# A token table from one-hot matmuls in place of scattered rows, with attention written out by group number and a lead of units that grows from 6 to 18

## What is computed

```python
x = L0_attn_x
x = x + layernorm(attention(layernorm(x)))
x = x + layernorm(ffn(layernorm(x)))

# attention: 16 heads of 16, keys and values from a latent of 64, causal
attn = softmax(where(causal_mask, -inf, einsum('bhtl,bsl->bhts', q_lat, c_kv) / sqrt(hs)))

# ffn: top 2 of 8 experts for each of the 4096 tokens
w, idx = top_k(xf @ Wg, 2);  w = softmax(w)
xhat = (xf - mu) * rsqrt(var + EPS)
h = relu((xhat * gamma[e] + beta[e]) @ W1[e] + b1[e])
out[e] = h @ W2[e] + b2[e] + xf
y[n] = sum over the two chosen e of w[n, e] * out[e][n]
```

## Time and profile before

| | us |
|---|---|
| median of 3 runs | 1285.25 (1284.64 to 1285.45) |
| the profiled execution | 1283.42 |
| its span, first to last instruction | 1281.8 |
| TensorE busy | 1054.5 (82%) |
| VectorE busy | 824.1 (64%) |
| ACT busy | 640.9 (50%) |
| POOL busy | 588.2 (46%) |

### The profile page before, as it was taken

One profiled execution on the slowest core, in us unless ns is written; L12 is line 12 of the kernel. 1 busy time (PEld: TensorE's weight loads), 2 busy tenths in 40 slices (PEclk: granted clock), 3 DMA queues, 4 the chain that ended last, 5 costly groups with the idle time before them and its releaser, 6 DMA issues. The chain is left out here.

```text
span 1281.8 us, 24447 instructions
## 1 busy us (share of the span) xinstructions
PE 1054.5 (82%) x7329; PEld 806.4 (63%) x7329; DVE 824.1 (64%) x2492; ACT 640.9 (50%) x1111; POOL 588.2 (46%) x675
## 2 busy tenths in 40 slices
PE   5979999999999999998533513999999999999900
PEld 2545555555555555554233513999999999999900
DVE  6739877777777777772188521556655655565577
ACT  2640666666666666666444422444444544454533
POOL 4214555555555555556747771223222222232237
PEclk9985999999999999999855555999999999999955
DMA  4994344545444444432261235142541414421173
GB/s 147 372 359 131 107 167 167 167 167 167 165 165 160 159 160 160 169 113 108 96 236 66 83 128 196 59 162 63 183 178 48 177 49 177 146 79 50 41 270 131
DMA packets 93849, 190.03 MB, mean 148 GB/s; under 512 B 27480, under 2 KB 58600, under 8 KB 85512
## 3 DMA queue, kind: packets, MB, share of 16 engines
q1 hardware_dynamic: 84508, 165.14, 37.0%
q0 software_dynamic: 7680, 22.09, 5.0%
q10 hardware_dynamic: 1588, 1.92, 0.5%
HBM read 109.54 MB, written 79.05 MB: 147 GB/s over the span
## 5 line engine op out<-in xcount | busy, mean ns | idle before, releaser
L778 ACT ACTIVATE att_pt<-att_ps_s 128x1024 f32<-128x1024 f32 (+3 forms) x384 | 297.9, 814 | 180.5 <-PE att_ps_s L693 176.8
L805 DVE CUSTOM_DVE_ANT_0 att_ps_m<-att_ps_m,keep_future 128x384 f32<-128x384 f32 (+2 forms) x384 | 204.3, 586 | 77.9 <-PE att_ps_m L656 77.9
L1521 ACT ACTIVATE moe_hf<-moe_ps_h,moe_b 128x256 f32<-128x256 f32 x288 | 134.4, 474 | 224.7 <-PE moe_ps_h L1477 215.3
L656 PE MATMUL att_ps_m<-att_k,att_q 128*128 128x512 f32 (+3 forms) x576 | 181.1, 389 | 5.1 <-DVE att_pm L805 3.9
L814 DVE TENSOR_REDUCE att_pm<-att_ps_m 128x1 f32<-128x512 f32 x256 | 161.4, 685 | 21.8 <-PE att_ps_m L656 21.7
L601 POOL TENSOR_SCALAR_AFFINE_SELECT att_pt<-att_pt 128x512 f32<-128x512 f32 x128 | 81.3, 636 | 186.8 <-ACT att_pt L778 186.8
L693 PE MATMUL att_ps_s<-att_q,att_k 128*128 128x512 f32 (+3 forms) x576 | 156.0, 360 | 6.3 <-ACT att_pt L778 5.2
L1430 POOL DMA_INDIRECT ys<-moe_o,moe_home x72 | 74.1, 1029 | 183.3 <-DVE moe_o L1560 170.4
L693 PEld LDWEIGHTS att_ps_s<-att_q,att_k 128*128 128x128 f32 x576 | 95.2, 188 | 56.5 <-issue 28.9
L1554 DVE TENSOR_TENSOR moe_hTl<-moe_hf,moe_hTh 128x256 fp32r<-128x256 f32 x288 | 124.1, 431 | 10.0 <-DVE moe_hTh L1552 0.2
L656 PEld LDWEIGHTS att_ps_m<-att_k,att_q 128*128 128x128 f32 x576 | 99.7, 195 | 47.9 <-DVE att_pm L805 15.1
(11 more groups left out here) (197 smaller groups left out, 2503.8 us busy)
## 6 DMA issues: line engine op xcount, KB each, us to landing
att_raw<-in_w SPq DMA_DIRECT2D x16, 1024.0 KB, 5.3
ws<-att_raw_hi SPq DMA_DIRECT2D x16, 1024.0 KB, 3.9
ws<-att_raw SPq DMA_DIRECT2D x16, 1024.0 KB, 5.8
moe_rows<-xs SPq DMA_DIRECT2D x38, 258.0 KB
att_q<-qs SPq DMA_DIRECT2D x33, 256.0 KB
att_k<-ks SPq DMA_DIRECT2D x66, 128.0 KB
weights_w_0h<-ws SPq DMA_DIRECT2D x8, 1024.0 KB
weights_w_0l<-ws SPq DMA_DIRECT2D x8, 1024.0 KB
```

Source lines behind the costliest of these rows:

```text
L656: ins = pe.matmul(out[:, end - keys:end], qg[slot][:, h // 2, i * P:(i + 1) * P], kg[slot][:, h, k0:k0 + keys], start=not whole, stop=not ...
L778: act.activation(pt[:, blk % NPT, 2 * p:2 * p + 2, off:CH], ps_s[k % 2][:, :, off:CH], ACT.Exp, scale=HS ** -0.5).then_inc(ex_done, 1)
L805: ins = dve.tensor_tensor_reduce(part, part, future[:, CH - keys:CH], 1.0, LOWEST, ALU.add, ALU.max, pm[:, g % 2, 0, head, place:place + 1])
L1521: act.activation(hf[:, f % NHB], ps_h[f % NHB][:], ACT.Relu, bias=b1[r][:, f:f + 1]).then_inc(hf_done, 1)
```

## The change

In words:

- attend is written out for 16 groups with constant numbers, without the loop over b and without registers. The turn is one job, and the lead of units of the next group is AHEAD = (6, 10, 14, 18): 6 before the first scores, and `DEALT_RISE` deals 42 units instead of 38 in each of the groups 0, 1 and 2. Three slots are left (NSL = 3), and the load of group g+2 is issued in group g. The first fetch of raw weights comes behind the load of group 2.
- route makes no slots. `route_xf` and `route_xh` come from ACT straight out of the attention's result (L1214 and L1220), with the turned copies between them; one set of moments of x and its normalised copy on VectorE are gone. The rows are written to HBM in the order of the tokens, by plain DMAs of SP. Rank and expert become a row and a column: per batch and choice POOL makes one-hot matrices (`make_low`, 16 of 128 columns, L946; `make_block`, 16 of 272 columns, L952), ACT scales the first ones by the token's number (`rows_of`, L1237 and L1239), and TensorE multiplies the two (`table`, 32 matmuls of 272 columns a batch), so that a PSUM bank holds for every expert and place the token that belongs there. For the last batch VectorE makes the low ones and half of the others. VectorE makes `home` and `token` of the table.
- experts: POOL reads the tile's column of the table and fetches the rows by two indirect DMAs, in front of the stores of the tile before; its places come by one copy from `home`. SP issues only biases and fills.

```diff
-NSL = NG
+NSL = 3
-HALF = NU // 4 * 2
+AHEAD = (6, 10, 14, 18)
+DEALT_RISE = ((2, 0), (1, 2), (1, 0), (2, 0), (2, 0), (1, 1), (2, 0), (1, 0), (2, 0), (1, 3), (2, 0), (2, 0),
...
-        extra = {7: [("out", 0, 0)], 15: [("out", 0, 1)], 17: [("turn", 1, 0), ("turn", 1, 1)]}.get(k, [])
...
+    first = [*units[:NU], ("turn", 0, 0), *units[NU:NU + AHEAD[0]]]
...
+                for g in range(GROUPS):
+                    if 0 < g < GROUPS - 2:
+
+                        sp.wait_ge(pv_done, g * NB)
+                        load_group(sp, d, slots, g + 2)
+                    if g + 1 < GROUPS:
+                        max_rows(g + 1)
+                    keep_split(g)
```

```diff
+        def make_low(eng, b):
...
+            for k in range(K):
+                for t in range(TB):
+                    ins = eng.tensor_scalar(at_low[:, k, t], cols[:, 0:P], low[:, k, t:t + 1], None, ALU.is_equal)
+            ins.then_inc(low_done, 1)
...
+        def make_block(eng, k):
...
+            for t in range(TB):
+                ins = eng.tensor_scalar(at_block[:, k, t], cols[:], cell[:, k, t:t + 1], None, ALU.is_equal)
+            ins.then_inc(block_done, 1)
...
+                def rows_of(b):
...
+                    for k in range(K):
+                        act.activation(low_row[:, k], at_low[:, k], ACT.Copy, scale=own_row[:, k:k + 1]).then_inc(rows_done, 1)
                     for t in range(TB):
...
+                        act.activation(low_tile[:, :, t], at_low[:, :, t], ACT.Copy, scale=float(K * P * (b * TB + t))
+                                       ).then_inc(rows_done, 1)
...
+                def table(b):
+
+                    pe.wait_ge(block_done, (b + 1) * K)
+                    out = ps_tab[:, 0:E * TABLE]
+                    for k in range(K):
+                        pe.wait_ge(rows_done, b * LOW_ROWS + k + 1)
+                        for t in range(TB):
+                            pe.matmul(out, low_row[:, k, t], at_block[:, k, t], start=(b + k + t == 0), stop=False)
```

```diff
-                fetch(d["xs"][0:XT, :].rearrange("(k p) c -> p k c", p=P))
-                second = tile_slots(1)
...
+                def gather(n):
+
+                    pool.tensor_copy(source[:], keep["token"][:, columns(n)]).then_inc(sourced, 1)
+                    pool.wait_ge(sourced, n + 1)
                     settle(pool, keep["passed"])
...
+                    for t in range(XT // P):
+                        pool.indirect_dma_start(rows[:, t], None, d["xs"],
+                                                bass.IndirectOffsetOnAxis(ap=source[:, t:t + 1], axis=0)).then_inc(rows_in, 16)
```

More of the change, by code:

```diff
@@ L444, with __init__, all, all_jobs @@
-class Step(list):
-    early = 0
-AFTER = bank_jobs()
-JOBS = sum(len(x) + len(y) for x, y in AFTER)
-assert JOBS % NBK == 0 and NB % NPT == 0
+class Step:
+    def __init__(self):
+        self.early, self.late = [], []
+    def all(self):
+        return self.early + self.late
+def all_jobs():
+    units = [("unit", g, m) for g in range(GROUPS) for m in range(NU)]
+    first = [*units[:NU], ("turn", 0, 0), *units[NU:NU + AHEAD[0]]]
+    number, units = len(first), units[NU + AHEAD[0]:]
+    groups = []
+    for g in range(GROUPS):
+        steps = []
+        turned = False
+        for k, (early, late) in enumerate(DEALT_RISE if g + 1 < len(AHEAD) else DEALT):
+            step = Step()
+            steps.append(step)
+            for jobs, count in ((step.early, early), (step.late, late)):
+                for _ in range(count):
+                    if units and (units[0][1] < g + 2 or units[0][1] == g + 2 and units[0][2] < ahead(g + 1)):
+                        jobs.append((units.pop(0), number))
+                        number += 1
+                if jobs is step.early:
+                    more = [("out", g, c) for c in range(2) if k == OUT_STEPS[c] and g + c > 0]
+                    if k > TB * 2 and not turned and g + 1 < GROUPS and (not units or units[0][1:] > (g + 2, 2)):
+                        more.append(("turn", g + 1, 0))
+                        turned = True
+                    for job in more:
+                        jobs.append((job, number))
+                        number += 1
+        groups.append(steps)
+    assert not units
+    return [(job, n) for n, job in enumerate(first)], groups, (("out", GROUPS, 0), number)
@@ L454, in attend @@
+GROUPS = B * NG
+FIRST, DEAL, LAST = all_jobs()
+NUMBER = {job: n for job, n in [*FIRST, *(j for steps in DEAL for step in steps for j in step.all())]}
 def attend(nc, d, keep, slots):
@@ L729, in _, with values_pass @@
[L729 to L733 removed]
+                def values_pass(g, k):
+                    for blk in PASSES[k]:
+                        if blk >= 0:
+                            values(g, blk)
+                        elif g > 0:
+                            values(g - 1, NB + blk)
+                pe.wait_ge(started, 1)
@@ L735, in _ @@
+                pe.matmul(ps_o[:], onesb[:, 0:P], onesb[:], start=True, stop=True)
+                jobs(FIRST)
+                for g, steps in enumerate(DEAL):
+                    for k, step in enumerate(steps):
+                        scores(g, k)
+                        jobs(step.early)
+                        if k in PASSES:
+                            values_pass(g, k)
+                        jobs(step.late)
+                values_pass(GROUPS, 1)
+                jobs([LAST])
             @block.scalar
@@ L790, in _ @@
-                for b in range(B):
-                    body(b)
-                keep_out(B, 0, 0)
-                keep_sums(B - 1, NG, 0, numbered(B - 1)[1])
+                fill_mt(0, NUMBER["turn", 0, 0])
+                for g, steps in enumerate(DEAL):
+                    for k, (c, j, p) in enumerate(STEPS):
+                        blk = g * NB + k // 2
+                        act.wait_ge(st_made, g * NS + k + 1)
+                        if blk >= NPT:
+                            act.wait_ge(pv_done, blk - NPT + 1)
+                        off = max(0, (j - c * TC) * P)
+                        act.activation(pt[:, blk % NPT, 2 * p:2 * p + 2, off:CH], ps_s[k % 2][:, :, off:CH],
+                                       ACT.Exp, scale=HS ** -0.5).then_inc(ex_done, 1)
+                        if k == 2 and g > 0:
+                            keep_out(g, 0)
+                        if k == 10:
+                            keep_out(g, 1)
+                        for what, n in steps[k].all():
+                            if what[0] == "turn":
+                                fill_mt(what[1], n)
+                            if what[0] == "out":
+                                keep_sums(g, what[2], n)
@@ L1027, in _ @@
+                for b in range(B):
+                    if b + 2 < B:
+                        roots_y(b + 2)
+                    table(b)
+                    if b + 2 < B:
+                        roots_x(b + 2)
             @block.vector
@@ L1384, in _ @@
                 first = firsts(sp)
-                each(sp, first, lambda q, r: None, tile, leave)
-                sp.wait_ge(rows_in, first[E] * 16 + 32)
-                settle(sp, keep["passed"])
+                for e in range(E):
+                    leave(e // 2, e % 2)
                 sp.wait_ge(o_free, first[E] + 1)
```

705 lines of the change are left out of this document (325 added, 380 removed).

## The result

The changed kernel takes 1309.85 us (median of 4, 1308.58 to 1310.76) against 1285.32 us (1284.64 to 1285.45): a ratio of 1.0189, 95% interval 1.0176 to 1.0202. I had forecast 1273 with a range of 1259 to 1289. The profiled span is 1307.8 against 1281.8, so 26.0 us have to be found.

The account below looks back on a forecast made before the run. TensorE bounds attention and experts, with most to gain in the routing gap between; -6.0 + 3.6 - 4.5 + 0 - 18.7 + 8.2 + 5 = -12.4 on 1283.42 gives 1271.0 profiled, 1273 as median, range 1259 to 1289.

Parts of the forecast that it names:

- part 5: Routing: scatters removed, POOL comparisons at 0.36 and 0.50 us added; experts start at 764.0 instead of 782.7, -18.7 us.
- the walk: Routing path followed along ACT, without holes if POOL keeps up; POOL becomes the bound above 1.05 us a pair.
- Rival (a): Routing: POOL's comparisons cost what two-input operations cost, 1.24 us a pair; kernel 1288 to 1293 us; chance 0.14.
- Rival (e): Routing: ACT's order holds it, y work of batch 3 waiting for POOL; 5 us more, 1278; chance 0.08.
- rival (b): Experts: gathers do not suffer from fills, in the first tile and later; -5 and -5, 1263 us; chance 0.12.
- rival (d): Attention: VectorE sets the pace in the first three groups, losing the early scores' saving; 1277 us; chance 0.08.
- Part 2: Attention, growing lead: four more units in each of groups 0, 1 and 2 cost +3.6 us (2.8 to 7.8).
- Part 3: Attention: the turn's second job, which computes nothing but takes a bank, goes in 15 groups; -4.5 us.
- Part 4: Attention: three slots instead of four, loads issued later with 0.7 to 1.5 us to spare; 0 us.
- Rival (c): Attention: every slot load is late by 0.7 us; kernel 1281 us; chance 0.08.
- Part 6: First expert tile: POOL's gathers land beside SP's 4 MB fill, 11.0 us after the stage's start; +8.2 us.
- Part 7: Later expert tiles beside six fills: gathers queued behind a store's landing come 0.8 us late each time; +5 us.

Follow-up runs that it names:

- run 3: Changed kernel with only the 128-column comparisons of batches 0 to 2 moved from POOL to VectorE: 1285.8 us, ratio 1.001 to the kernel before.
- run 2: Changed kernel with all comparisons of batches 0 to 2 moved from POOL to VectorE: 1277.9 us, ratio 0.9937 to the kernel before.
- Run 7: Changed kernel with comparisons of batches 0 to 2 on VectorE and gathers first, plus a lead of 18 units from the start: 1267.1 us.
- run 8: Changed kernel with comparisons of batches 0 to 2 on VectorE and gathers first, plus four slots and loads one group earlier: 1259.8 us, ratio 0.9813.
- run 5: Changed kernel with POOL's gather ahead of the wait for the last store, and SP's first fill behind the first gather: 1299.0 us.
- run 9: Unused bytes added: kernel before with 2176, 1285.6 us, with 32, 1293.3; run 8's kernel with 32, 1262.6; changed kernel with 96, 1307.1.
- run 1: Separate kernel without the reference's work, eight operations of each kind on POOL: tensor with scalar 0.60 us for 128 columns, 0.96 for 272.

## Why the prediction was wrong

**The step that failed** is in part 5: "I take 0.36 and 0.50, since the comparison is one-input and its pointer is read once." I priced it by a line through an operation of 8 columns and a copy of 1024. The copy is another kind of operation, 0.41 for 272 columns where the tensor with scalar takes 0.96. Of 8-column rows (0.24) nothing can be read on the price of a column.

The rest of the walk fits once the price is right. With batch 0's comparisons at 25.7 in place of 13.8 it has ACT go on at 670 + 25.7 + 4.2 + 2.7 = 702.6 where I had 690, and ACT went on at 703.04. With the small price my walk had 130 us of routing, and run 3, at 0.96 a pair, took 132.0. Its sharp edge at 1.05 did not hold: run 2 took 8 us less than run 3. The 18.7 us of gain were there, and more (25); POOL took back 31, by the comparisons' own time, at least 16 of it, and perhaps by the roots that stood behind them (run 2).

Rival (a) named the mechanism, but bounded the price by the two-input rows, 1.24; at 1.6 the time left my range, and its own. Nor did its turning point, 1.2 a pair for the kernel as a whole, hold: with the other losses below, the change broke even at 0.96 (run 3). Both prices came from rows of other kinds than the one in question, so neither was a bound. Two of my three signs of being wrong came true: comparisons took 0.78 on average, above 0.6, and ACT stood still for POOL in batch after batch. Rival (e), ACT's own order, fell with run 2; rival (b) fell with the first expert tile, whose gathers did wait beside the fill; rival (d) had the cost of the first three groups about right in size.

The Trainium skill (GPSIMD Engine Reference, 4.1 Engine selection) calls one-input operations on this engine roughly line-rate, and two-input ones about two times slower than VectorE's. Here the one-input tensor with scalar was the slower of the two kinds, 0.96 against 0.76, and VectorE did the same comparison in 0.28 (run 2, 4.41 for 16). By the 1.8 cycles of the Trainium skill (GPSIMD Engine Reference, 3.1 Elementwise, side-by-side cycle accounting), an estimate, 272 columns would be 0.65 us; the sum by that estimate, 1280, was nearer to the truth than mine, and still far.

**Part 1**, the early scores: -6.0 forecast, -5.5 measured, -6.5 from the stage's own start, which came 1.1 later. Right.

**Part 2**, the growing lead: mis-sized, +3.6 against 7.9, the upper bound that I had worked out (7.8). Run 7 gives the size: 3.1 from the first scores to the second turn (26.56 against 23.48), then 2.4 and 2.5. The +7.4 above is the same less what part 3 wins in these groups. Why four units cost that is open: the waits that the profile shows are only 0.4 us longer in the group from 152.50 to 185.93 than in one of 31.04 (0.97 and 0.58), while TensorE is busy for 32.45 us in place of 30.46, both at a granted clock of 1.00.

**Part 3**, the empty job: -4.5 forecast for fifteen groups; 0.38 in each of twelve is -4.6, and the first three are inside the +7.4. Right.

**Part 4**, three slots: I took 0 with a margin of 0.7 to 1.5 us. It held in eight groups and failed in four, 2.7 us (run 8: 3.0). Rival (c) was right in kind, a third of its size.

**Part 6**: +8.2 against +8.0, by the mechanism named (run 5). **Part 7**: +5 against +7.8; the waits themselves are 5.4, and the periods behind them add the rest. Run 5 removes all of it. **Part 8** was +0.1.

**Not in the sum**: 4 us from buffer addresses (run 9). No row of before could have told it.

Together: 24.6 us missed in routing, 6.9 in attention, 2.8 in tiles beside fills and 4.0 for addresses are 38.3, and 1271.0 + 38.3 is 1309.3; the changed kernel's profiled run took 1309.4.

## What to carry to other kernels

Price an operation by rows of its own kind at two sizes; where the trace has none, say that there is no bound, and measure it alone before the plan is built on it. When work moves to an engine, ask which short operations others wait for stand behind it in its order. A prefetch and a gather want to be issued ahead of waits and of bulk loads; and after any change of buffers compare the pitch of untouched matmuls, since that can move by 1 to 2%.

## What the runs showed of the hardware

- GpSimd: a tensor with a scalar costs 0.28 us + 2.5 ns a column at 128 partitions (602 and 960 ns, run 1), 0.07 less with a constant; of the types tried (f32 and bf16) none changed it. A copy of 272 columns is 0.41, two tensors 0.76. Beside two-input operations of VectorE the comparison took 1.25 in place of 0.96. VectorE makes it in 0.20 and 0.28 (run 2).
- TensorE: the place of buffers in SBUF, by as little as 32 bytes, moved the time of a tile of 100 matmuls from 11.72 to 11.94 with nothing else changed (run 9). Which relation between addresses counts is open: 32 bytes past a multiple of 64 was not the rule.
- Indirect reads of 256 rows of 1 KB land 1.8 us after their issue ends (run 5), and 6.3 us after it when 4 MB have been issued beside them (first tile of the changed kernel, 793.11 to 799.41).
- The granted clock: the same 32 matmuls of a table took 6.62 us at 0.57 and 5.38 at 0.71, in kernels with the same routing (run 8).
